# Pixel attention: scores as waves of four 32-row products in one ring of seven PSUM banks

## The reference

```python
# layer 0: one head of 32 channels per image, then attention over 128 concepts
score = jnp.einsum('bcn,bcm->bnm', th, ph)         # [1024, 1024], c = 32
lat = jnp.einsum('bnm,bcm->bnc', softmax(score), g)
# layer 1: a class map and gates (small)
# layer 2: group norm, then 8 heads of 32 channels per image
weight = jnp.einsum('bct,bcs->bts', q * scale, k * scale)   # per head
a = jnp.einsum('bts,bcs->bct', softmax(weight), v)
out = x + w_proj @ a + b_proj
# layer 3: group norm, attention over the 8 heads of one pixel, projection
```

## Time and profile before

| | us |
|---|---|
| median of 3 runs | 2235.7 |
| profiled execution | 2227.61 |
| its span | 2225.8 |
| PE busy | 1979.0 (89%) |
| DVE busy | 1531.2 (69%) |
| POOL busy | 1029.1 (46%) |
| ACT busy | 827.0 (37%) |

### The profile page before, as it was taken

How to read it: one execution, slowest core, us unless ns; L and a number is a source line. 1 busy time by engine, 2 the same in 40 slices (tenths; PEclk the granted TensorE clock), 3 DMA queues, 4 the chain that set the end, 5 groups by cost and what they waited for, 6 DMA issues and landing times.

```text
span 2225.8 us, 36373 instructions
## 1 busy us (share of the span) xinstructions
PE 1979.0 (89%) x12212; PEld 1015.5 (46%) x12212; DVE 1531.2 (69%) x2315; ACT 827.0 (37%) x1546; POOL 1029.1 (46%) x437
## 2 busy tenths in 40 slices
PE   6999685799999999999999999999999969888885
PEld 2443232354554554544544544545544335445442
DVE  6766647787666777676777766777666127888786
ACT  0152310004544544443544443544545613333320
POOL 0243210005455355454454444454444608788787
PEclk8799888789999999999999999999999979999996
DMA  7200020232330330330330330330331020122211
GB/s 219 58 2 1 1 85 27 57 115 62 77 77 20 78 79 21 77 79 20 77 79 20 77 79 20 77 79 20 78 77 39 2 97 25 63 65 66 79 46 60
DMA packets 89664, 132.53 MB, mean 60 GB/s; under 512 B 58180, under 2 KB 58486, under 8 KB 89462
## 3 DMA queue, kind: packets, MB, share of 16 engines
q1 hardware_dynamic: 79958, 129.36, 21.1%
q10 hardware_dynamic: 9504, 0.59, 0.3%
HBM read 44.83 MB, written 25.17 MB: 31 GB/s over the span
## 4 chain that ended last, share of the span: by engine, by line
PE 71%; DVE 16%; issue 4%; DMA 4%; ACT 2%; SPq 2%; POOL 1%; POOLq 0%; DVEq 0%; ACTq 0%
PE AV L650 11%; PE S L637 11%; PE RB L621 11%; PE S L621 5%; PE SUM L660 4%; PE RB L689 4%; PE RB L885 3%; DVE MX L1276 3%; SPq L443 2%; PE AV L898 2%; PE RB L766 2%; DVE ENC L1617 2%; DVE DEV L1316 2%; PE RB L706 2%; PE RB L934 1%
## 5 line engine op out<-in xcount | busy, mean ns | idle before, releaser
L1276 DVE TENSOR_REDUCE MX<-RB 128x1 f32<-128x512 f32 x783 | 515.2, 684 | 89.3 <-PE RB L621 80.7
L1014 ACT ACTIVATE PR<-S 128x512 f32<-128x512 f32 x640 | 356.5, 597 | 578.3 <-PE S L637 559.0
L1175 POOL TENSOR_TENSOR ACC<-PR 128x1024 f32<-128x1024 f32 x72 | 170.3, 2373 | 760.6 <-ACT PR L1014 758.7
L637 PE MATMUL S<-QS,KS 98*128 98x512 f32 x1152 | 470.2, 460 | 17.4 <-issue 8.5
L1175 POOL TENSOR_TENSOR ACC<-ACC,PR 128x1024 f32<-128x1024 f32 x152 | 360.0, 2371 | 198.2 <-ACT PR L1014 189.4
L621 PE MATMUL RB<-KS,QS 96*128 96x512 f32 x783 | 393.1, 524 | 32.7 <-DVE MX L1276 20.1
L1014 ACT ACTIVATE X<-S 128x512 f32<-128x512 f32 x512 | 283.7, 597 | 284.0 <-PE S L637 277.2
L621 PEld LDWEIGHTS RB<-KS,QS 96*128 96x128 f32 x783 | 245.0, 318 | 251.6 <-DVE MX L1276 153.0
L637 PEld LDWEIGHTS S<-QS,KS 98*128 98x128 f32 x1152 | 222.4, 198 | 218.5 <-issue 93.6
L1276 DVE TENSOR_REDUCE MX<-S 128x1 f32<-128x512 f32 x369 | 251.7, 682 | 32.2 <-PE S L621 27.0
L621 PE MATMUL S<-KS,QS 96*128 96x512 f32 x369 | 186.3, 505 | 11.4 <-DVE MX L1276 6.8
(11 more groups left out here) (235 smaller groups left out, 2096.3 us busy)
## 6 DMA issues: line engine op xcount, KB each, us to landing
X<-out_y SPq DMA_DIRECT2D x24, 1024.0 KB, 5.1
QS<-HI SPq DMA_DIRECT2D x144, 128.0 KB, 2.4
KS<-HI SPq DMA_DIRECT2D x144, 128.0 KB, 2.5
out_y<-X SPq DMA_DIRECT2D x16, 1024.0 KB, 4.1
QS<-LO SPq DMA_DIRECT2D x72, 128.0 KB, 2.6
KS<-LO SPq DMA_DIRECT2D x72, 128.0 KB, 2.4
X<-in_x SPq DMA_DIRECT2D x8, 1024.0 KB, 8.7
OHU<-out_y SPq DMA_DIRECT2D x8, 512.0 KB, 4.4
```

Source lines behind the costliest of these rows:

```text
L637: mm(ST[:, (H * s + h) % BANKS, :], KS[par][:, h, P * mt:P * mt + P], QS[par][:, h, HALF * half:HALF * half + HALF], start=True, stop=True ...
L1014: nc.scalar.activation(exps(i, s, pair)[:, HALF * one:HALF * one + HALF], ST[:, (H * s + h) % BANKS, :], ACT.Exp, scale=1.0 if i is None e ...
L1175: nc.gpsimd.tensor_tensor(ACC[:, pair, :], so_far, exps(i, s, pair), ALU.add).then_inc(pool_used, 1)
L1276: nc.vector.tensor_reduce(out=MX[:, h, t, half:half + 1], in_=bank(), op=ALU.max, axis=AX.X).then_inc(ring_free, 1)
```

## The change

Every score is now made by four products on 32 rows, HI·HI, HI·LO, LO·HI and ones times the maxima's rows. A head's channels lie on their own 32 partitions, so the four heads use four row strips of the array and can be issued as a wave; the next wave adds to the same banks. HI and LO are kept per unit (two buffers) and no stacks are copied. Maxima are made from HI·HI alone, also in waves of four heads; the same number of reductions, 64 a unit. Only a query half's maxima (8 waves) are made ahead: the second half's are made in the first half of the unit's own window. After eight waves VectorE negates and splits them (`negate`), TensorE transposes them, and VectorE spreads them over 32 rows with a selector (`flip`), in steps 7 and 15, before which nothing of the next half may start (`all_read`).

All products but P·V share one ring of seven banks in the order in which they are issued, the sums' too. GpSimd adds six key tiles of eight instead of five; TensorE sums the last two and GpSimd's total in one job at the start of the next half. The next unit's query, key and value products move to steps 1 to 4, 6 and 9 of each window, the output products to 5, 7, 10 and 11. In each step all other jobs come first and the wave of maxima last. The kernel's tail keeps its order; it gets other buffers.

```diff
-BANKS = 3
-POOL_TILES = (0, 1, 2, 4, 5)
+SLOTS = 7
+TILES_HALF = MT // 2
+POOL_TILES = (0, 1, 2, 3, 4, 5)
...
+class Ring:
+    def place(self):
+        self.at += 1
+        return self.slots[(self.at - 1) % len(self.slots)]
...
+def maxima(half):
+    return [("max", half, t, keys) for t in range(TILES_HALF) for keys in range(2)]
...
+def window_jobs(post=False, nxt=True, gn=False, trail=True, pad=0):
     jobs = [[] for _ in range(STEPS)]
+    late = [[] for _ in range(STEPS)]
+    for half in range(2):
+        first = MT * half
+        if half == 1 or trail:
+            jobs[first].append(("sums",))
+            jobs[first + SPREAD_AT].append(("spread", half - 1))
+        if half == 0 or nxt:
+            tiles = maxima(1 - half)
+            jobs[first].insert(0, tiles[0])
+            for n, tile in enumerate(tiles[1:]):
+                late[first + n].append(tile)
+            jobs[first + MT - 1].append(("negate", 1 - half))
...
     if nxt:
+        for n in range(4):
+            jobs[1 + n].append(("qk", n // 2, n % 2))
+        jobs[6].append(("v", 0))
+        jobs[MT + 1].append(("v", 1))
+    if post:
+        jobs[5].append(("post", 0, 0))
+        jobs[7].append(("post", 1, 0))
+        jobs[MT + 2].append(("post", 0, 1))
+        jobs[MT + 3].append(("post", 1, 1))
     if gn:
+        jobs[6].append(("stats",))
+        jobs[MT + 2].append(("gn", 0))
+        jobs[MT + 4].append(("gn", 1))
+    for half in range(2):
+        if half == 0 or nxt:
+            jobs[MT * half + MT - 1].append(("flip", 1 - half))
+    return [early + after for early, after in zip(jobs, late)]
...
-START = []
-for _h in range(H):
-    START += [("max", _h, _t, _half) for _t in range(MT) for _half in range(2)]
-    START += [[("v", 1)], [("qk", 0, 0)], [("qk", 0, 1), ("qk", 1, 0)], [("qk", 1, 1)]][_h]
+START = [("v", 0)] + maxima(0)[:4] + [("v", 1)] + maxima(0)[4:] + [("negate", 0), ("flip", 0)]
...
-        RING = [S4[:, BANKS, :], RB[:, 0, :], RB[:, 1, :]]
+        RING = [S4[:, n, :] for n in range(4)] + [RB[:, 0, :], RB[:, 1, :], SUM[:, :]]
...
-            def stacks(u, par):
...
-            def rows(u, par):
...
+            def fill(reader, tally, back):
+                slot = ring.place()
+                if slot in held:
+                    sem, counted, k = held[slot]
+                    wait(pe, sem, counted.base + k)
+                held[slot] = (reader, tally, tally.k - back)
+                return RING[slot]
...
+            def max_scores(u, par, half, t, keys):
+                if half == 0 and t == 0 and keys == 0:
+                    wait(pe, stage_ready, u + 1)
+                first = HALF * half + P * t
+                for h in range(H):
+                    mm(bank(), HI[par][D * h:D * h + D, 0, first:first + P],
+                       HI[par][D * h:D * h + D, 1, HALF * keys:HALF * keys + HALF],
+                       start=True, stop=True).then_inc(ring_full, 1)
...
+            def scores(u, par, s):
                 half, mt = s // MT, s % MT
+                if mt == 0:
+                    all_read()
+                keys, cols = slice(P * mt, P * mt + P), slice(HALF * half, HALF * half + HALF)
+                dst = []
+                for h in range(H):
+                    row = slice(D * h, D * h + D)
+                    exped.add()
+                    dst.append(fill(exp_done, exped, 0))
+                    mm(dst[h], HI[par][row, 1, keys], HI[par][row, 0, cols], start=True, stop=False,
+                       skip_group_check=True)
+                for h in range(H):
+                    row = slice(D * h, D * h + D)
+                    mm(dst[h], HI[par][row, 1, keys], LO[par][row, 0, cols], start=False, stop=False,
+                       skip_group_check=True)
...
+                for h in range(H):
+                    row = slice(D * h, D * h + D)
+                    mm(dst[h], ONER[row, :], NMR[row, half, :], start=False, stop=True,
+                       skip_group_check=True).then_inc(st_full, 1)
...
+            def sums(n):
+                kept.add(2)
+                dst = fill(half_kept, kept, 1)
+                for mt in (MT - 2, MT - 1):
+                    for h in range(H):
+                        mm(dst[D * h:D * h + D, :], ONES[:, 0:D],
+                           exps(mt, h // 2)[:, HALF * (h % 2):HALF * (h % 2) + HALF],
+                           start=(mt == MT - 2), stop=False)
+                wait(pe, pool_used, 2 * POOL_SUMS * (n + 1))
...
+            def row_max(half, t, keys):
+                for h in range(H):
+                    nc.vector.tensor_reduce(out=MX[:, h, t, keys:keys + 1], in_=bank(), op=ALU.max,
+                                            axis=AX.X).then_inc(ring_free, 1)
+            def negate():
+                own()
+                link(nc.vector.tensor_reduce(out=NM[:, :, :], in_=MX[:, :, :, :], op=ALU.max, axis=AX.X,
+                                             negate=True))
+                link(nc.vector.tensor_copy(NMX[:, :, 0:TILES_HALF], NM[:, :, :]))
...
```

More of the change, by code:

```diff
@@ L51, with __init__ @@
 class Tally:
-    def __init__(self, banks=BANKS):
-        self.base, self.k, self.banks, self.first = 0, 0, banks, 0
+    def __init__(self):
+        self.base, self.k = 0, 0
     def add(self, n=1):
@@ L400, in program, with iteration @@
         block = ctx.enter_context(nc.Block())
-        def iteration(i, window, tallies, turns=None):
+        def iteration(i, window):
             u = 2 * i + 2
@@ L406, in iteration @@
             first = isinstance(i, int) and i == 0
-            window(u, 0, window_jobs(post=not first, prep=not last, gn=not last), i)
-            window(u + 1, 1, window_jobs(prep=not last, nxt=not last, gn=last), i)
-        RING_PER = 2 + 2 + 4 + 2 + 4 + 64 + 2 + 2 + 4 + 64
+            window(u, 0, window_jobs(post=not first, gn=not last, trail=not first, pad=0 if first else PAD), i)
+            window(u + 1, 1, window_jobs(nxt=not last, gn=last), i)
+        TURNED = [job for step in window_jobs(post=True, gn=True) + window_jobs() for job in step]
+        PAD = -(2 * EXPS + sum(places(job, False) for job in TURNED)) % SLOTS
+        RING_PER = sum(places(job, False) for job in TURNED if job[0] != "sums")
         TURNS = B - 2
@@ L586, in _, with carry @@
         def _(pe):
-            ring = Tally()
+            ring = Ring()
+            drained, exped, kept = Tally(), Tally(), Tally()
+            held = {}
             pe_need = Tally()
             mm = nc.tensor.matmul
-            def bank():
-                wait(pe, ring_free, ring.add() - ring.banks)
-                return RING[ring.slot()]
+            def fill(reader, tally, back):
[5 more added lines that the diff above has]
+                return RING[slot]
+            def bank():
+                drained.add()
+                return fill(ring_free, drained, 0)
+            def carry():
+                for slot, (sem, counted, k) in held.items():
+                    held[slot] = (sem, counted, k - counted.k)
             def all_read():
-                wait(pe, ring_free, ring.now())
+                wait(pe, ring_free, drained.now())
             def qk_l0(g, which, half):
@@ L947, in _ @@
                 front_qk(0, unit)
-            for o in range(CT):
-                for half in range(2):
+            for half in range(2):
+                for o in range(CT):
                     output_product(o, half, B - 1)
@@ L1357, in run @@
                             after(0, job)
-                for s in range(STEPS):
-                    run(jobs[s][0:3])
-                    if s == (1 if par == 1 and i is None else INVERT_AT) and trail:
+                    if s == (1 if early else INVERT_AT) and ("sums",) in jobs[0]:
                         invert(2 * u - 1)
```

470 lines of the change are left out of this document (217 added, 253 removed).

## The result

| | before | after |
|---|---|---|
| median, us | 2234.3 (4 runs, 2230.8 to 2237.5) | 2414.8 (4 runs, 2408.0 to 2419.3) |
| span of the profiled execution | 2225.8 | 2406.2 |
| PE busy | 1979.0 | 1960.8 (81%) |
| DVE busy | 1531.2 | 1502.6 (62%) |
| granted clock in the loop | 0.99 | 0.93 |

The changed kernel takes 1.081 times as long (95% interval 1.077 to 1.084). Forecast were 2326 us, slower, in a range of 2205 to 2490. The sign and the mechanism came out; the size was 89 us short, so that the change costs 180 us, twice the 90 forecast.

What follows compares the result with a forecast made beforehand. TensorE was taken to bound the loop, VectorE close behind. Stage changes summed to +65 us (2291), the clock added 25 (span 2316), and the median was forecast at 2326 us, 4 per cent slower, range 2205 to 2490.

Steps and rivals of the forecast that it cites:

- the release: In each step, the next scores' second wave waits until VectorE drains the other product and reduces one maximum; plain step 3.4 us.
- The step list: Times for the loop's 32 steps by kind, worked from release to release: 175.9 us an iteration against 165.1, +10.8.
- the start and the last image: Until first exponential -33 us, layer 0 windows +4 and +13, preparation -25; last iteration +32, tail untouched.
- rival D: Input transfers, not maxima, bound the start: -33 becomes -6, up to +27 us; no chance of its own.
- the first iteration: Without sums at its start and without output products: 166.3 us, +9.
- the iteration: One loop iteration of 32 steps: 175.9 us against 165.1, +65 over six iterations.
- the clock's: Loop clock 0.97 instead of 0.99, four per cent of the time at 1.2 GHz: +25 us over 1,500 us.
- the forecast's own neighbourhood: Whole-kernel times of 2240 to 2400 us around the forecast of 2326; chance 0.50.
- B: Score waves do not fully share the array: 2533 us with two strips at once, 2948 all serial; chance 0.13.
- C: Loop clock falls to 0.87, a quarter of the time at 1.2 GHz: 2466 us; chance 0.14.
- The case of B that gave 2407: Four row strips give 3.07 times one, from the Trainium skill, so a wave is 0.31 us: 2326 + 81 us.
- Rival A: About one wave left after the release, 0.24 to 0.4 us off each of 288 steps: say 2190 us; chance 0.20.

Runs made afterwards that it cites:

- experiment 1: Changed kernel with the wave of maxima ahead of the step's other jobs in every step but 0 and 8: 2189.8 us, ratio 0.982 to the kernel before.
- experiment 9: Experiment 7's kernel with the wave of maxima put back last in each step: 2324.4 us, ratio 1.045 to the kernel before.
- experiment 8: Changed kernel, maxima last, with extra products issued while TensorE waits for VectorE: 2410.0 us, ratio 1.082; a microsecond at half clock cost 0.41 to 0.47.
- experiment 5: Experiment 1's kernel with group norm's small operations rewritten to have one operand in PSUM: 2132.1 us, ratio 0.957 to the kernel before.
- experiment 7: Experiment 5's kernel, spread-maxima wait before the fourth wave, statistics and group sums later, step 7's maxima transposition and spreading before the output product: 2045.0 us, ratio 0.917.
- the repairs: Group norm's operations in PSUM, later wait for the spread maxima, statistics moved to steps 9 and 10; on the changed kernel with maxima first: 2045.0 us.
- experiment 11: Kernel before the change with experiment 5's rewritten group norm operations: 2186.2 us, ratio 0.982.

## Why the prediction was right, and short by 89 us

*Right: the release.* The step list was worked from one wait, the next scores for VectorE's first maximum. Measured against forecast, in steps at full clock: query 6.33 (6.2), values 5.87 (5.6), plain 3.40 (3.4), inverse 4.93 (4.7), inverse with output 6.50 (6.5), sums 6.54 and 6.55 (6.8; the other two, 7.08 and 7.40, hold time at half clock), second group sum 3.71 (3.6). Experiments 1 and 9 show the mechanism by undoing it, 225 and 279 us.

*Right: the start and the last image.* First exponential at 55.7 us (56), which excludes rival D; by like events the two windows of layer 0 and the preparation are +11, +14 and -28 (+4, +13, -25), so that the first iteration starts 37 us sooner (41); last image +33 (+32). The tail, which I called untouched, is 8 shorter.

*Short: the first iteration*, +25 for +9, between the starts of its first P·V and of the next one's. It holds 22.1 us at half clock, where the one before the change held 3.4.

*Short: the iteration, 194.5 for 175.9.* By the same steps, the 18.6 us are:

- 7.7 in six steps that hold a half-clock stretch: three query steps of 6.88, 7.63 and 7.34, where the others are 6.33, the inverse of the second window (5.80 for 4.7, elsewhere 4.93), and two output steps (6.89 and 7.75 for 5.45 each). P·V in such a stretch has its eight in 1.94 us, at full clock 1.06:

```profile
1047.44 1.94 PE L680 MATMUL AV<-PR,VT 128*32 128x512 f32 x8
```

- 3.7 at the loop's end. The step list had a plain flip there; TensorE stands idle 3.54 us while it turns the loop round, 2.8 of them after VectorE is done. The waves behind it run at half clock. The 165.1 of before have such a turn in them, with 1.90 idle (first line; the other two are of after), while the list for after had none:

```profile
973.36 0.49 PE L637 MATMUL S<-QS,KS 98*128 98x512 f32 x1 [1.90 <-issue]
...
1209.22 0.69 DVE L1326 TENSOR_TENSOR NMR<-SUM,CST 128x512 fp32r<-128x512 f32 x1 [0.42 <-PE SUM L642]
1212.72 1.13 PE L656 MATMUL S<-HI 32*128 32x512 f32 x4 [3.54 <-issue]
```

- 2.5 at the first window's last flip. GpSimd holds a cast of 16 columns for 2.31 us there, 1.4 more than the 0.87 of the sum; the rest goes with the waves behind it, which run at half clock. The 0.87 was a mean of two kinds: of the 72 casts of before the median is 0.17, and the longest, held by GpSimd, 4.15:

```profile
1118.49 4.69 POOL L1212 TENSOR_TENSOR ACC<-ACC,PR 128x1024 f32<-128x1024 f32 x2
...
1120.89 2.31 DVE L1318 CAST NMX<-NM 128x16 fp32r<-128x16 f32 x1
```

- 2.5 for statistics and first group sum (9.87 and 9.47 for 8.6 and 8.25), 1.0 for eight query steps at 0.13, 0.8 for value steps (a self-wait of 0.22 behind the bias), 0.4 for the others.

*The failed term is the clock's.* "I take 0.97" and "+25" stood for all stages; the loop got 0.93, that is 26.6 us at half clock in each iteration. The first item alone is 7.7 in each of the loop's six iterations, 46 us, and six other steps of the list hold time at half clock too. By experiment 8's price of 0.41 to 0.47 the 22.7 us more than before are 9 to 11 us an iteration (an estimate), 56 to 64 in six, where 25 stood for all stages. The rule by which the 25 was made (118 of 176 us are TensorE's and double, so 0.40 is lost of each microsecond at half clock) agrees with that price; it was the share that was wrong.

I set the share by TensorE's busy time, 0.96 to fall to something between. TensorE was busy 0.84 of the new loop, and what it had between were waits. Of the half clock of an iteration three quarters lie behind single waits of 2.4 to 3.8 us, and one quarter, the stretch of the row at 1047.44 and its like, behind three or four query steps in a row with a wait of 0.97 each. In the loop of before VectorE held TensorE up for 1.5 us at most at a time, and a stack's DMA once for 2.8, with 3.4 us at half clock behind it. That the waits cause the stretches was seen, not shown: the time at half clock falls as the waits do (26.6 us an iteration after, 20.5 in experiment 9, 15.7 in experiment 5, 6.1 in experiment 7, 3.9 in the kernel before). Experiment 8 speaks for it in part: at the query steps of the second window, whose waits the fillers covered whole, the stretch is gone in four of five iterations, but the one of the first window's query steps stayed, and the one at the turn of the windows doubled, from 3.4 to 6.8.

*Luck.* The 2415 us lie above the forecast's own neighbourhood (2240 to 2400). They are in the range because rivals B and C had stretched it, and neither came. The case of B that gave 2407 is nearest, by chance: its dearer wave did not happen, a wave was 0.23 to 0.24.

*Rival A* (under 5.2 us a step) had no part: the mean step was 6.08. Its idea, that little is left behind the release, fails on rows like 1165.08: three further waves follow it. *Rival C's* clock, 0.87, was not reached.

## What to carry to other kernels

Where two engines pass banks round a common ring, write the place of each product in a step and ask which of its readers the next step's last bank comes from. Work that drains slowly belongs first in a step, so that its reader runs beside the rest: here that order alone was worth 225 to 279 us of 2400, more than the 180 that the whole change lost; with it and the repairs the new layout was 6.5% faster than the old one. And price each step from release to release, with the loop's turn and the half clock as terms of their own.

## What was not expected of the hardware

- A small VectorE operation with both operands in SBUF waits for GpSimd's running instruction to end. On two columns it takes 0.16 us alone, up to 2.36 beside additions of 2.36, and 4.44 (at most 4.63) beside products of 4.9. In the traces of the kernels before and after and of experiments 1, 5, 7 and 11, each one that started beside such an instruction ended 0.01 to 0.04 us behind it or, twice, behind the next one. So did the casts of the negated maxima, which have only one operand.
- The same arithmetic with one operand in PSUM took 0.16 to 0.17 each time, and the split's passes and the maxima, which read PSUM, kept their 0.75 and 0.68. Nor is everything held that reads SBUF: beside the same additions the reduction of 32 columns took its 0.19, the reciprocal its 0.24 and the statistics their 0.68.
- The hold moves with the timing: a repair of one place (experiment 5) put it at another, where it cost part of the gain.
- Four 32-row products of fp32r on four row strips, each to a bank of its own, 128 columns of weights and 512 moving, cost 0.235 us together, as one does.
- At the turn of the hardware loop TensorE was idle for 3.5 to 3.7 us (in experiment 7 up to 3.9), and for 1.5 to 1.9 before. Why it grew was not tested.
